# Gated linear attention in one pass: queries and keys scaled by VectorE out of PSUM, and matmuls laid on quadrants of the array

## The chip, the cores and the metric

The kernel runs on one core of one Trainium2 chip. The metric is the device time of one execution in microseconds (us). Engines are named as the profile names them: PE is TensorE, DVE VectorE, ACT ScalarE, POOL GpSimd, SP SyncE. L1649 is line 1649 of the kernel.

## The reference, cut to what matters

The kernel computes a whole decoder of four layers on x of 32 sequences x 128 positions x 128 features, in float32. The change touches one sublayer, the attention of layer 2: a gated linear attention with 16 heads of 64 and chunks of 64 positions, so two chunks a sequence.

```python
def chunk_gla(q, k, v, alpha, C=64):          # q and k were scaled to length one per head
    log_a = jnp.log(jnp.maximum(alpha, 1e-06))
    la_cum = jnp.cumsum(log_a, axis=3)
    la_mean = la_cum.mean(-1)
    decay = jnp.exp(la_mean[..., :, None] - la_mean[..., None, :]) * tril
    attn_intra = jnp.einsum('bhncd,bhnmd->bhncm', q, k) * decay
    o_intra = jnp.einsum('bhncm,bhnmd->bhncd', attn_intra, v)
    decay_to_end = jnp.exp(la_cum[:, :, :, -1:, :] - la_cum)
    kv_chunk = jnp.einsum('bhncf,bhnce->bhnfe', k * decay_to_end, v)
    q_dec = q * jnp.exp(la_cum)
    ...                                        # state S, from zero: o = q_dec @ S, then S * chunk_decay + kv_chunk
    return (o_intra + o_inter).reshape(B, Hh, N, D)
```

The state starts at zero and there are two chunks, so chunk 0 needs o_intra alone, and chunk 1 adds its decayed queries times kv_chunk of chunk 0. q, k, v and the gate are projections of the layer-normalised x to 1024 columns. alpha is a sigmoid, and its logarithm is made as -ln(1 + exp(-g)). The result is projected back to 128 features, and x is added.

## The kernel before, in words

All layers run one after the other; each ends with a barrier over all engines. The attention of layer 2 is the function gla. The function decoder calls it through chunks("c", ...), once for each of PASSES = 4 groups of NB = 8 sequences ("batches"); between the calls lies the barrier.

A call first normalises its eight batches: DVE computes statistics and applies them with scale and shift (lines 68 to 91), ACT takes the root (L107), PE transposes (L59), ACT copies the result into xt_c (L1705). Only then does the loop start.

The loop is software-pipelined by a list written out by hand. ORDER (in the head of gla) goes over c and names for each c the steps of three batches: the front part of batch c + 2, the middle of c + 1, the back of c. Names in capitals are units: PE writes a unit's result into a pair of PSUM banks, of which there are four in a ring, so unit k waits until the pair of unit k - 4 was freed. Every engine walks the same list in order and does its own part of each name; each serves its queue strictly in that order. The units of a period are G, QD, Q, QT, S1, K, KT, ES, O, DF, V, OT, SC, OUT:

- G, Q, K, V (L1649): projections of one batch, two matmuls of 512 columns each. The profile shows two records for each float matmul that is not a transposition.
- For Q and K, ACT squares out of PSUM (SQ, L1716); DVE copies the raw values out (QN, KN, L1819), which frees the pair, and sums the squares per head (L1820) and clips (L1823). After both, ACT takes Ln (L1724) and Exp (L1729), which gives RN, one over the length; POOL multiplies QN and KN by it (L1794).
- For G, DVE adds the bias and clips (L1809, L1811), ACT takes Exp and Ln (L1719, L1722), DVE negates and clips (L1826) and sums per head (L1831, into LM).
- QT, KT (L1655): eight transposes each of the scaled queries and keys; ACT and DVE copy them out (L1741, L1836).
- ES (L1659): cumulated log gates by a matmul with a constant; ACT's Exp makes EX; POOL multiplies queries and keys with it into KQ (L1783, L1785).
- DF (L1664): differences of the means; ACT's Exp and POOL's triangle (L1788) make DEC.
- SC (L1670): scores; DVE multiplies by DEC (L1844, L1845). QD (L1675) transposes the decayed queries of chunk 1; S1 (L1679) makes the state of chunk 0.
- O (L1687, L1688): the output of both chunks; ACT copies it (L1762), OT (L1692) transposes it, DVE copies (L1855), OUT (L1696) projects, DVE adds x (L1858).

## Time and profile before

| | us |
|---|---|
| median of 3 runs | 4913.18 (4910.89 to 4914.86) |
| the profiled execution | 4913.76 |
| its span | 4912.0 |
| the layer, from its first to its last instruction | 847.2 |

The span is the time from the first to the last instruction. The layer lies from 2169.8 to 3017 us in it. In timelines a row is a run of equal instructions (x is their count), merged; the number behind the start is the time from the first one's start to the last one's end, so with PE, whose matmuls overlap, the distance between starts of neighbouring rows tells what a unit costs. A bracket at the end gives the idle time before a row and what ended it.

### The profile page before, as it was taken

To read this page: it belongs to the slowest core of one execution; us is meant where nothing else is said; L and a number is where in the kernel's file an instruction comes from. 1 tells how busy PE (TensorE), PEld (TensorE's weight loads), DVE (VectorE), ACT (ScalarE), POOL (GpSimd) and SP (SyncE) were. 2 spreads that over 40 slices of the span, in tenths; PEclk is the share of its full clock that TensorE was granted. 3 is DMA by queue.
4 is the path that set the end of the run, shared out by engine and by line. 5 is a ranking of instruction groups with operands and counts; after the bars stand their busy time and mean duration, and the time that the engine had idled before them with its cause. 6 is when DMAs were issued, how large, how long until landed. Compare 5 with 4: busy or idle time off the path is not lost. (4 is left out here: it accounts for less than half of the span.)

```text
span 4912.0 us, 79412 instructions
## 1 busy us (share of the span) xinstructions
PE 3958.9 (81%) x30626; PEld 2747.9 (56%) x30626; DVE 3057.8 (62%) x7919; ACT 2146.5 (44%) x3375; POOL 1238.5 (25%) x803
## 2 busy tenths in 40 slices
PE   0788888787998789879898897654549999598998
PEld 0466666565565566646565655443436777365665
DVE  9577777566899567577666674985352112466545
ACT  4466666443222245436565465541123344354222
POOL 2444444222343211015454453321000000010000
PEclk9999999997999679889999998776579999799999
DMA  2222222000000010000000000003300000000000
GB/s 87 49 48 48 49 47 42 4 1 1 1 1 1 1 50 2 1 1 1 1 1 1 1 1 1 14 20 109 99 13 1 1 1 1 27 2 2 1 1 18
DMA packets 58267, 91.98 MB, mean 19 GB/s; under 512 B 15410, under 2 KB 42500, under 8 KB 56132
## 3 DMA queue, kind: packets, MB, share of 16 engines
q1 hardware_dynamic: 53620, 80.09, 7.0%
q10 hardware_dynamic: 4272, 6.81, 0.4%
q8 instruction: 245, 4.01, 0.3%
q14 instruction: 130, 1.06, 0.1%
HBM read 42.69 MB, written 10.62 MB: 11 GB/s over the span
## 5 line engine op out<-in xcount | busy, mean ns | idle before, releaser
L844 PE MATMUL banks<-XT,weight_region 128*128 128x512 f32 x1696 | 798.0, 610 | 0.0
L866 PEld LDWEIGHTS banks<-weight_region,HT 128*128 128x128 f32 x4672 | 576.8, 196 | 136.9 <-issue 111.1
L1123 DVE SCALAR_TENSOR_TENSOR x_res<-banks,WT,x_res 128x128 f32<-128x128 f32 x1056 | 297.4, 344 | 519.8 <-PE banks L866 466.6
L866 PE MATMUL banks<-weight_region,HT 128*128 128x128 f32 x4672 | 581.7, 280 | 14.2 <-DVE HT L1111 8.7
L844 PEld LDWEIGHTS banks<-XT,weight_region 128*128 128x128 f32 x1696 | 312.0, 197 | 295.3 <-issue 290.6
L945 ACT ACTIVATE HT<-banks,weight_region 128x512 f32<-128x512 f32 x256 | 174.3, 687 | 269.3 <-PE banks L844 263.0
L1649 PE MATMUL banks<-weight_region,xt_c 128*128 128x512 f32 x512 | 256.1, 631 | 5.9 <-DVE KNT L1836 3.2
L458 DVE TENSOR_REDUCE MX<-banks 128x8 f32<-128x1152 f32 x128 | 173.2, 1353 | 115.6 <-PE banks L275 113.7
L384 ACT COPY PT<-banks 128x384 f32<-128x384 f32 x384 | 171.5, 481 | 132.0 <-PE banks L285 130.3
L1502 ACT COPY PT<-banks 77x512 f32<-77x512 f32 x256 | 143.1, 582 | 189.4 <-PE banks L1424 189.4
L999 POOL TENSOR_TENSOR T<-T,T 128x512 f32<-128x512 f32 x128 | 162.9, 1274 | 216.5 <-ACT T L968 214.2
L968 ACT ACTIVATE T<-T 128x512 f32<-128x512 f32 x128 | 80.4, 630 | 275.9 <-DVE T L1100 275.8
L59 PE MATMUL banks<-sb_c_ident,XN 128*128 128x128 f32 x96 | 26.5, 432 | 200.8 <-DVE XN L91 163.9
L961 ACT ACTIVATE T<-banks 128x512 f32<-128x512 f32 x128 | 76.1, 597 | 244.1 <-PE banks L844 244.0
L285 PE MATMUL banks<-sb_c_ident,SM 128*128 128x128 f32 x1152 | 178.4, 282 | 4.6 <-ACT PT L384 2.7
L427 POOL TENSOR_TENSOR KT<-KT,FL 128x512 f32<-128x512 f32 x64 | 81.3, 1271 | 373.4 <-DVE FL L447 373.4
L1513 POOL MEMSET VZ<- 77x4160 f32 x2 | 7.1, 3562 | 663.7 <-POOLq L48 663.7
L258 PE MATMUL banks<-XT,weight_region 128*128 128x256 f32 x512 | 144.0, 411 | 29.0 <-ACT PT L384 24.8
L399 ACT ACTIVATE SM<-SM 128x1152 f32<-128x1152 f32 x128 | 150.3, 1174 | 29.2 <-DVE SM L466 29.2
L1424 PE MATMUL banks<-sb_c_ident,SM 128*77 128x128 f32 x1024 | 162.3, 293 | 0.0
L1086 DVE TENSOR_TENSOR HT<-banks,T 128x512 f32<-128x512 f32 x128 | 87.9, 690 | 111.9 <-PE banks L844 98.2
L466 DVE TENSOR_TENSOR SM<-banks,MX 128x1024 f32<-128x1024 f32 x128 | 155.4, 1214 | 0.0
(452 smaller groups left out, 9137.8 us busy)
## 6 DMA issues: line engine op xcount, KB each, us to landing
FL<-RAW SPq DMA_DIRECT2D x512, 64.0 KB, 2.3
T<-s4d_k_dram SPq DMA_DIRECT2D x8, 1024.0 KB, 6.0
weight_region<-in_l_ffn__w_dram SPq DMA_DIRECT2D x2, 2048.0 KB, 7.7
film_dram<-F SPq DMA_DIRECT2D x8, 512.0 KB, 2.9
weight_region<-in_l_ffn__w_dram ACTq DMA_DIRECT2D x2, 2048.0 KB
film_out<-film_dram SPq DMA_DIRECT2D x3, 1024.0 KB, 6.5
x_res<-in_x_dram SPq DMA_DIRECT2D x1, 2048.0 KB
weight_region<-in_l_ffn__w_dram SPq DMA_DIRECT2D x2, 1024.0 KB, 9.7
```

The costliest lines, as they stand in the source:

```text
L285: ins = nc.tensor.transpose(ring(item, n)[:, q * P:(q + 1) * P], SM[:, n % 3, 3 * c + q, :], E.ident)
L384: nc.scalar.copy(PT[:, n % 2, 3 * c:3 * c + 3, :].rearrange("p h q -> p (h q)"), ring(f"T{c}", n)[:, 0:3 * P]).then_inc(s.pt, 1)
L399: nc.scalar.activation(SM[:, n % 3], SM[:, n % 3], ACT.Exp, scale=SCALE).then_inc(s.ex, 1)
L458: nc.vector.tensor_reduce(MX[:, n % 2], sc, AXX, ALU.max).then_inc(s.mx, 1)
L466: nc.vector.tensor_tensor(SM[:, n % 3, 1:9, :].rearrange("p (a i) k -> p i a k", a=2), sc[:, :, :, 0:P], bc(MX[:, n % 2].unsqueeze(3), [P, ...
L844: nc.tensor.matmul(PS[:, q % 4, :], w, xt, start=True, stop=True).then_inc(s.h_ps, 1)
L866: ins = nc.tensor.matmul(PS[:, 4 + u % 2, b * P:(b + 1) * P], HT[:, u % 2, j, b * P:(b + 1) * P], w2[j], start=j == 0, stop=j == len(w2) - 1)
L945: ins = nc.scalar.activation(HT[:, u % 2, j, :], PS[:, (first[u] + j) % 4, :], ACT.Gelu, bias=W.b1[:, e, j:j + 1]).then_inc(s.act_done, 1)
L999: nc.gpsimd.tensor_tensor(T1[:, k % 2, :], T1[:, k % 2, :], T2[:, k % 2, :], ALU.mult).then_inc(s.gs, 1)
L1123: ins = nc.vector.scalar_tensor_tensor(R[:, t, :], PS[:, 4 + u % 2, b * P:(b + 1) * P], WT[:, t, e:e + 1], R[:, t, :], ALU.mult, ALU.add)
L1424: ins = nc.tensor.transpose(bank_of("T", k)[0:L, c * P:(c + 1) * P], SM[:, t % 3, 4 * c + a, :], E.ident)
L1649: ins = nc.tensor.matmul(pr[:, a * 512:(a + 1) * 512], E.xt[:, t * P:(t + 1) * P], w[:, a * 512:(a + 1) * 512], start=True, stop=True)
```

## The change

gla is called once and goes over all 32 batches; layer norm becomes three more names in ORDER, once for four batches: st (DVE statistics), ap (ACT: Ln and Exp for the root, POOL a small product, ACT four scalings) and X (PE transposes, ACT applies scale and shift per partition, since features are partitions then). E.r is no longer a chunk of r_all.

The weights of the four projections are reordered on the host so that the even heads fill columns 0 to 511 and the odd ones 512 to 1023 ("halves" o = 0, 1). The units Q and K become K1 and K2, each with four matmuls whose stationary operand is one chunk of 64 positions: K1 holds the keys of chunk 0 and the queries of chunk 1, on swapped partition halves for odd heads, and K2 the rest. ACT squares them, DVE sums and clips, ACT takes Ln and Exp for each alone (r1, r2), and DVE multiplies out of PSUM into T1 and T2 (r1, r2), which is what frees the pair of banks. T1 and T2 are transposed (units of the same names), and ACT copies both out. KQ is one product of T1 and EX on POOL. V, ES and DF write their second half in two column halves of the array, so that odd heads lie on swapped partitions. SC, QS (in place of QD and S1) and O consist of matmuls of 64 x 64 with 64 columns, spread over the four quadrants of the array; O is computed transposed, its second part behind a wait of PE for its own semaphore o1, and OT is DVE's copy of it. There are 12 units a period and not 14, and one X in four periods. ACT preloads one table set for Exp and Ln. The log gates keep their positive sign, the constants carry the minus; the clip of the gate changes its bound so that the later clip is not needed. The memsets go, since no operand is padded with zeros any more.

```diff
@@ -1584,112 +1584,160 @@
...
-    ORDER = []
-    for c in range(-2, NB):
-        for n, t in (("G", c + 2), ("QD", c), ("Q", c + 2), ("QT", c + 1), ("S1", c), ("K", c + 2), ("e", c + 2), ("KT", c + 1),
-                     ("ES", c + 1), ("O", c), ("l", c + 2), ("DF", c + 1), ("r", c + 2), ("V", c + 2), ("OT", c), ("SC", c + 1), ("OUT", c)):
-            if 0 <= t < NB:
...
+    ORDER = [("st", 0), ("ap", 0), ("X", 0)]
+    for c in range(-2, B_ALL):
+        for n, t in (("G", c + 2), ("QS", c), ("K1", c + 2), ("T1", c + 1), ("r1", c + 2), ("e", c + 2), ("K2", c + 2), ("T2", c + 1), ("r2", c + 2), ("l", c + 2),
+                     ("ES", c + 1), ("O", c), ("s", c + 2), ("DF", c + 1), ("V", c + 2), ("SC", c + 1), ("OUT", c), ("rt", c + 2)):
+            if 0 <= t < B_ALL:
                 ORDER.append((n, t))
...
+        for n, lead in (("st", 3), ("ap", 2), ("X", 1)):
+            if (c + 2 + lead) % GB == 0 and 0 < (c + 2 + lead) // GB < NG:
+                ORDER.append((n, (c + 2 + lead) // GB))
...
+                    elif n in ("K1", "K2"):
+                        kc = 0 if n == "K1" else 1
+                        for o in range(2):
+                            for w, k_ in ((W.wk, kc), (W.wq, 1 - kc)):
+                                ins = nc.tensor.matmul(pr[rows(k_ ^ o), cols(o)], chunk[k_], w[:, cols(o)], start=True, stop=True)
+                    elif n == "V":
+                        nc.tensor.matmul(pr[:, cols(0)], x, W.wv[:, cols(0)], start=True, stop=True)
+                        for k_ in range(2):
+                            ins = nc.tensor.matmul(pr[rows(1 - k_), cols(1)], chunk[k_], W.wv[:, cols(1)], start=True, stop=True)
+                    elif n in ("T1", "T2"):
+                        pe.wait_ge(s.n1 if n == "T1" else s.n2, t + 1)
+                        src = (T1 if n == "T1" else T2)[:, t % 2]
                         for j in range(NJ):
                             ins = nc.tensor.transpose(pr[:, j * P:(j + 1) * P], src[:, j * P:(j + 1) * P], E.ident)
-                    elif n == "ES":
...
+                    elif n in ("ES", "DF"):
+                        if n == "ES":
+                            pe.wait_ge(s.lg, t + 1)
+                            m, v = E.gla_sum, LA[:, t % 2]
+                        else:
+                            pe.wait_ge(s.rt, t + 1)
+                            m, v = E.gla_after, RT[:].rearrange("p h c -> p (h c)")
+                        nc.tensor.matmul(pr[:, cols(0)], m, v[:, cols(0)], start=True, stop=True)
+                        for k_ in range(2):
+                            ins = nc.tensor.matmul(pr[rows(1 - k_), cols(1)], m[:, rows(k_)], v[:, cols(1)], start=True, stop=True)
...
+                            for o in range(2):
+                                for key, query, b in ((T1T, T2T, o), (T2T, T1T, 1 - o)):
+                                    ins = nc.tensor.matmul(pr[rows(b), HALF * o + C * j:HALF * o + C * (j + 1)],
+                                                           key[rows(o), j, rows(b)], query[rows(o), j, rows(b)], start=True, stop=True)
...
+                    elif n == "QS":
+                        pe.wait_ge(s.kqd, t + 1)
+                        pe.wait_ge(s.va, t + 1)
+                        for j in range(NJ):
+                            for o in range(2):
+                                at = HALF * o + D * j
+                                nc.tensor.matmul(pr[rows(o), C * j:C * (j + 1)], KQ[rows(1 - o), at:at + D], E.ident[rows(1 - o), rows(1 - o)], start=True, stop=True)
+                                ins = nc.tensor.matmul(pr[rows(o), HALF + D * j:HALF + D * (j + 1)], KQ[rows(o), at:at + D], VA[rows(o), t % 2, at:at + D],
+                                                       start=True, stop=True)
                     elif n == "O":
...
+                            for k_ in (1, 0):
+                                for o in range(2):
+                                    at = HALF * o + D * j
+                                    ins = nc.tensor.matmul(pr[rows(o), HALF * k_ + C * j:HALF * k_ + C * (j + 1)], VA[rows(k_ ^ o), t % 2, at:at + D],
+                                                           AT[rows(k_ ^ o), o, j, :], start=k_ == 0 or j == 0, stop=k_ == 0)
+                        ins.then_inc(s.o1, 1)
+                        pe.wait_ge(s.o1, t + 1)
+                        for j in range(NJ):
+                            for o in range(2):
+                                ins = nc.tensor.matmul(pr[rows(o), HALF + C * j:HALF + C * (j + 1)], S1[rows(o), j, :], QDT[rows(o), j, :],
+                                                       start=False, stop=j == NJ - 1)
...
+                nc.scalar.preload_act_table_set(EXP_LN)
...
+                        nc.scalar.activation(SQ[:, 0], pr, ACT.Square).then_inc(s.sq1, 1)
...
+                    elif n == "r1":
+                        act.wait_ge(s.mx1, t + 1)
+                        nc.scalar.activation(SS[:, p, 0], SS[:, p, 0], ACT.Ln, scale=2.0 ** 40).then_inc(s.ls1, 1)
+                        act.wait_ge(s.ls1, t + 1)
                         if t >= 2:
-                            act.wait_ge(s.kn, t - 1)
...
-                        nc.scalar.activation(RN[:, p], SS[:, p], ACT.Exp, scale=-0.5, bias=E.ln2_20[:]).then_inc(s.rn, 1)
...
+                        nc.scalar.copy(VA[:, p], pr).then_inc(s.va, 1)
...
+                        nc.gpsimd.tensor_tensor(KQ[:].rearrange("p (o j d) -> p o j d", o=2, d=D), by_half(T1[:, p]),
+                                                EX[:].rearrange("p (o j d) -> p o j d", o=2, d=D), ALU.mult).then_inc(s.kqd, 1)
...
-                            nc.gpsimd.tensor_tensor(x, x, bc(RN[:, p, i, :].unsqueeze(2), [P, H, D]), ALU.mult).then_inc(done, 1)
...
-                        nc.vector.tensor_copy((QN if n == "Q" else KN)[:, p], pr).then_inc(s.qc if n == "Q" else s.kc, 1)
...
+                    elif n == "r1":
+                        dve.wait_ge(s.rn1, t + 1)
+                        if t >= 2:
+                            ready(dve, ("T1", t - 2))
+                            dve.wait_ge(s.kqd, t - 1)
+                        nc.vector.tensor_tensor(by_half(T1[:, p]), pair(("K1", t)).rearrange("p (o j d) -> p o j d", o=2, d=D),
+                                                bc(RN[:, p, 0, :].rearrange("p (o j) -> p o j", o=2).unsqueeze(3), [P, 2, NJ, D]), ALU.mult).then_inc(s.n1, 1)
...
+                        nc.vector.tensor_copy(OT[:].rearrange("p j (k c) -> p k j c", k=2), pr.rearrange("p (k j c) -> p k j c", k=2, c=C)).then_inc(s.ot, 1)
...
-                        nc.vector.tensor_tensor(AT0[0:C], prh[0:C], DEC[0:C], ALU.mult)
-                        nc.vector.tensor_tensor(LH[C:P], prh[C:P], DEC[C:P], ALU.mult).then_inc(s.at, 1)
...
+                        nc.vector.tensor_tensor(AT[:].rearrange("p o j c -> p (o j c)"), pr, DEC[:].rearrange("p h c -> p (h c)"), ALU.mult).then_inc(s.at, 1)
...
-        chunks("c", ("l2_attn", gla, nothing))
+        run("l2_attn", gla)
...
-    c["a_gla_sum"] = (same & np.where(q < 64, p > q, p <= q)).astype(f)
+    c["a_gla_sum"] = -(same & np.where(q < 64, p > q, p <= q)).astype(f)
```

## Rows read from the trace of the kernel before

**Rows 1.** Page, part 1: busy time (share of the span) and instructions of each engine.
```profile
PE 3958.9 (81%) x30626; PEld 2747.9 (56%) x30626; DVE 3057.8 (62%) x7919; ACT 2146.5 (44%) x3375; POOL 1238.5 (25%) x803
```
**Rows 2.** Windows of the layer: stretch, us, busy per engine, granted clock, DMA share, GB/s.
```profile
2169.80:2391.00 221.20, 187.80 (x1676) 125.80 (x1676) 148.09 (x177) 125.10 (x137) 111.18 (x54) 0.94 0.00 1
...
sum 847.20, PE 745.30 PEld 501.02 DVE 560.55 ACT 494.93 POOL 426.93; mean PE 186.32 PEld 125.26 DVE 140.14 ACT 123.73 POOL 106.73
```
**Rows 3.** Timeline of PE, one steady period: start us, us, engine, line, operation.
```profile
2308.51 1.08 PE L1675 MATMUL banks<-sb_c_ident,KQ 64*64 64x64 f32 x16
...
2311.34 1.04 PE L1655 MATMUL banks<-sb_c_ident,QN 128*128 128x128 f32 x8
2312.31 2.08 PE L1679 MATMUL banks<-V,KQ 128*64 128x64 f32 x32
2314.31 1.98 PE L1649 MATMUL banks<-weight_region,xt_c 128*128 128x512 f32 x4
2316.14 1.04 PE L1655 MATMUL banks<-sb_c_ident,KN 128*128 128x128 f32 x8
2317.01 1.88 PE L1659 MATMUL banks<-LA,sb_a_gla_sum 128*128 128x512 f32 x4
2318.82 0.27 PE L1687 MATMUL banks<-V,AT 128*64 128x64 f32 x1
...
2320.84 1.98 PE L1664 MATMUL banks<-RT,sb_a_gla_after 128*128 128x512 f32 x4
...
2325.34 1.97 PE L1670 MATMUL banks<-QB,KNT 128*64 128x128 f32 x32
2327.91 2.02 PE L1696 MATMUL banks<-weight_region,OT 128*128 128x128 f32 x16 [0.60 <-DVE OT L1855]
2329.76 1.88 PE L1649 MATMUL banks<-weight_region,xt_c 128*128 128x512 f32 x4
2331.58 1.08 PE L1675 MATMUL banks<-sb_c_ident,KQ 64*64 64x64 f32 x16
```
**Rows 4.** Timelines of ACT and DVE in that period: the norm of the queries.
```profile
2311.54 1.03 ACT L1716 ACTIVATE SQ<-banks 128x1024 f32<-128x1024 f32 x1 [0.91 <-PE banks L1649]
...
2312.60 1.23 DVE L1819 COPY QN<-banks 128x1024 f32<-128x1024 f32 x1 [0.21 <-ACT SQ L1716]
2313.74 1.21 DVE L1820 TENSOR_REDUCE SS<-SQ 128x16 f32<-128x1024 f32 x1
...
2319.78 0.18 DVE L1823 TENSOR_SCALAR SS<-SS 128x32 f32<-128x32 f32 x1
...
2324.34 0.22 ACT L1724 ACTIVATE SS<-SS 128x32 f32<-128x32 f32 x1
...
2326.79 0.31 ACT L1729 ACTIVATE RN<-SS,sb_c_ln 128x32 f32<-128x32 f32 x1
```
**Rows 5.** Groups of instructions by line: busy us, mean ns | idle before, releaser.
```profile
L1722 ACT ACT_TABLE_LOAD x32 | 41.1, 1283 | 0.6
...
L1472 ACT ACT_TABLE_LOAD x2 | 2.6, 1283 | 4.5 <-PEq L48 4.5
...
L1785 POOL TENSOR_TENSOR KQ<-KN,EX 64x1024 f32<-64x1024 f32 x32 | 77.6, 2424 | 2.5
```
**Rows 6.** Timeline of DVE: first G, last result of pass 1, first G after.
```profile
2186.30 1.23 DVE L1809 TENSOR_TENSOR LA<-banks,weight_region 128x1024 f32<-128x1024 f32 x1 [5.66 <-PE banks L1649]
...
2381.24 0.29 DVE L1858 TENSOR_TENSOR weight_region<-banks,x_res 128x128 f32<-128x128 f32 x1 [2.21 <-PE banks L1696]
...
2398.52 1.22 DVE L1809 TENSOR_TENSOR LA<-banks,weight_region 128x1024 f32<-128x1024 f32 x1 [5.66 <-PE banks L1649]
```
**Rows 7.** Timeline of PE in other layers: four row groups, four column groups.
```profile
514.51 0.77 PE L275 MATMUL banks<-KT,QT 32*128 32x144 f32 x16
...
1904.16 0.40 PE L1439 MATMUL banks<-PT,OZ 77*32 77x128 f32 x8
1904.38 0.40 PE L1437 MATMUL banks<-PT,VZ 77*32 77x128 f32 x8
```

## What the change should do to the time, predicted before it was run

> **What bounds the kernel now.** I read the page's busy shares first [rows 1]: PE is busy for 81% of the span, but that is a mean over a dozen layers, and the change touches one. The windows over that layer come next. It takes 847.2 us in four passes of eight batches, and PE is busy for 745.3 us of it, DVE for 560.6, ACT for 494.9, POOL for 426.9 [rows 2]; per batch that is 23.3, 17.5, 15.5 and 13.3 us. In the first pass the granted clock is 0.94, so most of it runs at 2.4 GHz.
>
> A busy PE can still wait, so I laid out one steady period from the timeline of PE, start of unit to start of unit [rows 3]. The unit QD starts at 2308.51 and again at 2331.58: a batch costs 23.07 us. Inside it the units stand shoulder to shoulder: a projection (four records of 512 columns) takes 1.82 us (G, 2329.76 to 2331.58), eight transposes 0.97 (2311.34 to 2312.31), S1 2.00 (2312.31 to 2314.31), ES 1.81 (2317.01 to 2318.82), O 2.02 (2318.82 to 2320.84), OUT 1.85 (2327.91 to 2329.76). The only gap is the 0.60 us before OUT. So in the steady state PE's own work is the bound; what DVE, ACT and POOL do matters only where it comes too late for PE.
>
> The second cost is the ramp. The first evacuations of G in two successive passes lie at 2186.30 and 2398.52 [rows 6]: 212.22 us, against 8 x 23.07 = 184.56. Each pass thus pays 27.66 us for its layer norm in front, for filling and for draining: the last result of the first pass is written at 2381.24, and 17.3 us pass before the next evacuation of G. Four ramps are 110.6 us. Check: 32 x 23.07 + 110.6 = 848.8, against 847.2 measured.
>
> **The change, part by part.**
>
> *One pass in place of four.* Layer norm goes into the loop (units st, ap, X, once in four batches), and three of the four ramps go: 3 x 27.66 = 83.0 us. Of the one that stays, the front gets shorter, because one group of four batches has to be normalised ahead of the first projection and not two. I take 21 us for the ramp; its ends are 28 (as now) and 16. What X costs PE in return is four transposes a group, 1.08 us, so 0.27 us per batch. ACT and DVE do the rest of the norm after their last unit of an iteration and ahead of the next G, with several us to spare.
>
> *PE's list.* The units OT, Q, K, QT, KT become K1, K2, T1, T2; OT goes, because O is now computed already transposed; QD and S1 become one unit QS. By the rows of before [rows 3]: G, K1, K2 at 1.82 are 5.46. V, ES and DF keep their columns, but their second half is issued as two column halves, which changes the tiling of the array once more inside the unit. Where a full unit is followed by a tiled one now, eight transposes take 0.97 us, against 0.87 before a full unit (2316.14 to 2317.01), so I add 0.1 to each: 3 x 1.92 = 5.76. T1 and T2 are 2 x 0.97 = 1.94, OUT 1.85, X 0.27. Sum: 15.28.
>
> *The quadrant units QS, SC and O.* Their matmuls are 64 x 64 with 64 columns, laid out over all four quadrants of the array. There are 32, 32 and 48 of them, and a float matmul leaves two records: 64, 64 and 96. No row of before shows four 64 x 64 tiles at once. The rows nearest to it are of three kinds. One tile at a time: S1, 32 records in 2.00 us, 62.5 ns each. Two column halves at once: O, 64 records in 2.02 us, 31.6 ns each [rows 3]. Four at once: 16 records of 144 columns in four row groups, in 0.77 us of which the last 0.28 is one record's own duration, 31 ns a record, and eight records on four column groups every 0.22 us, 27.5 ns a record of 128 columns [rows 7]. Both of the last are what the columns alone cost when four run together (128 columns on four tiles), so four tiles do run together, by rows as by columns, and the ends of my price are 14 ns (64 columns at that rate) and 62.5 ns. I take 17 ns, one slot of about 66 ns for four, near the 60 ns that a slot of two takes in O. QS and SC are then 64 x 17 = 1.09, with the switch 1.15 each. O has 64 records at 17 (1.09), a wait of PE for its own semaphore (a drain, about 0.3, the duration of one record), then 32 records on two quadrants only, 32 x 30 = 0.96: 2.3 with rounding down. Together 4.6.
>
> *The wait that is new.* Today the PSUM pair of Q or K is freed by a DVE copy that runs right behind SQ [rows 4]. In the change it is freed by the product r1 (or r2), behind a chain over two engines. The ring has four pairs, so the pair of K1 is wanted by ES, and that of K2 by DF. Count from the end of K1: ACT starts SQ 0.20 later (2311.34 to 2311.54) and needs 1.03; DVE reduces, 1.21, and clips, 0.18; ACT's Ln 0.22 waits at most for T1's copy, which ends at 2.25 while the clip ends at 2.65; Exp 0.31; then r1 on DVE, for which the copy out of PSUM of the same size stands, 1.23 [rows 4]. With 0.04 for each handing over that is 4.5, and 0.15 more until PE starts: 4.65. PE meanwhile has T1, K2, T2: 3.76. So PE stands for 0.9 us ahead of ES, in every period. Queued behind r1 on DVE is K2's reduction, and ACT runs e between; K2's chain ends about 8.5 us after K1, and DF is due at about 10.7, so that one costs nothing. The bounds of this stall are 0 and about 2.9 (below).
>
> *What else moves.* ACT loses the table loads, 1.28 us each, 32 of them on L1722 alone [rows 5]; a preloaded table set covers Ln and Exp in another layer, that of L1472, with 2 loads in all [rows 5]. It also loses the copy of O and a half of V's. DVE loses a copy, the negation of LA and half of S1. POOL loses the two normalising products, and its two products into KQ, 2.4 us each [rows 5], become one. I make that about 14, 11 and 7 us per batch for DVE, ACT and POOL, so none of them becomes the bound. I cost these savings at nothing, because PE covers them today and still does. The latest of their results is AT, which needs POOL's DEC: ACT has its part at about 12.0 us after K1's end, and one product of POOL's takes 2.4, so DEC is there at 14.4 and AT at 15.7; PE wants it freed for the next K1 at about 19.
>
> *Sum.* 15.28 + 4.6 + 0.9 = 20.8 us a batch, 2.3 less than now. Over 32 batches 666, with the ramp 687, against 847.2: 160 us less. The profiled execution took 4913.76 us, 0.6 above the median of the three runs and 1.8 above its own span; 4913.76 - 160.6 = 4753.
>
> **The rivals.**
>
> *A: the chain ahead of ES is longer.* It passes ACT, DVE, ACT, DVE, and both serve their queues strictly in order: if S1's copy or the clip of G is late, K1's reduction is late, and e or T1's copy can slip in ahead of Ln. One such slip is a unit of about 1 us on each engine, 2 us together: a stall of 2.9, a period of 22.8, 32 x 22.8 + 21 = 751, time 4817. For it: two slips would be enough. Against it: each engine is idle for a third of the period. Chance 0.17.
>
> *B: the quadrants run in pairs and not in fours.* In QS and O the two row halves of the array write the same PSUM bank, on different partitions; in the four-row-group rows each group has a bank of its own [rows 7], so nothing in the trace shows this sharing. If it keeps them apart, the rate is that of two tiles, 31.6 ns. QS and SC are 2.02 each, O 3.03 + 0.3: 7.4 in place of 4.6, a period of 23.6, 776 in all, time 4842. Chance 0.20. The Trainium skill speaks for it: its page TensorEngine Tiling (Array Packing), Restrictions and Gotchas, says that different row tiles cannot access the same PSUM bank at the same time; by that rule a kernel with this layout would lose the concurrency in QS and O. No row here bears on it either way.
>
> *C: slower than before.* The quadrant records run one after another at the 62.5 ns of S1. 224 records are then 14.0 us and not 4.3, the period 30.5, the layer 997, the time 5064. It decides against the change from a period of 25.8 on, where 32 periods and the ramp are 847: that is 5.0 us over 224 records, about 42 ns for each on average. For it: no row has four quadrants. Against it: rows and columns overlap separately in the trace, so both mechanisms would have to fail. Chance 0.05.
>
> **How the numbers follow.** Forecast 0.55: 4753, its own range 4710 (no stall, quadrants at 14 ns, a ramp of 16) to 4790 (a stall of 1.7, a ramp of 28). A 0.17, B 0.20, C 0.05; 0.03 for the rest, split between much better and no change. To leave out no more than 2 in 10 the range must take in B: 4710 to 4850. Faster by over 0.2% (about what a measurement of this kernel can tell from no change) 0.93, within it 0.02, slower 0.05.
>
> **What would show it.** In the profile after: no second layer norm front inside the layer; in the timeline of PE, QS and SC of 1.1 to 1.2 us each (2.0 would be B, 4.0 C) and O of 2.3; an idle time of about 0.9 us on PE ahead of ES, ended by DVE's r1 (2.9 would be A) and none ahead of DF; ES, V and DF no longer than 1.92; one table load for the layer; POOL near 7 us a batch. What would make the prediction wrong at its root is a period set by something other than PE, or a full-array unit that gets longer because its halves are tiled.

## The result, and the profile after

The changed kernel takes 4756.65 us (median of 4 runs, 4754.77 to 4757.61) against 4914.02 before: a ratio of 0.9677, 95% interval 0.966 to 0.9693, 157.4 us less. The prediction said 4753. Its profiled execution took 4756.02 us with a span of 4754.2.

The layer now runs from 2166.8 us to 2858.7 us: 691.9 us, against 847.2 [rows 2]. That is 155.3 of the 157.4 us. First the window over it (columns as in [rows 2]), which answers to the four passes of before:

```profile
2166.80:2860.00 693.20, 654.56 (x9440) 348.01 (x9440) 383.48 (x490) 356.92 (x506) 212.23 (x106) 0.99 0.01 2
```

PE is busy for 94% of it, and the granted clock is 0.99, so nearly all of it runs at 2.4 GHz. Per batch DVE, ACT and POOL are busy for 12.0, 11.2 and 6.6 us; the prediction had 14, 11 and 7. Next the timeline of PE, one period from the end of K1 to the end of the next K1, with the unit X in it. It answers to [rows 3]:

```profile
2397.52 1.09 PE L1697 MATMUL banks<-sb_c_ident,T 128*128 128x128 f32 x8
2398.55 1.94 PE L1688 MATMUL banks<-weight_region,XT 128*64 128x512 f32 x8
2400.41 1.09 PE L1697 MATMUL banks<-sb_c_ident,T 128*128 128x128 f32 x8
2402.03 1.12 PE L1705 MATMUL banks<-LA,sb_a_gla_sum 128*128 128x512 f32 x2 [0.52 <-DVE T L1905]
...
2404.10 1.16 PE L1733 MATMUL banks<-AT,VA 64*64 64x64 f32 x64
2405.35 1.15 PE L1739 MATMUL banks<-QDT,S 64*64 64x64 f32 x32
2406.43 1.12 PE L1705 MATMUL banks<-RT,sb_a_gla_after 128*128 128x512 f32 x2
...
2408.49 1.12 PE L1690 MATMUL banks<-weight_region,XT 128*128 128x512 f32 x2
...
2410.55 0.27 PE L1714 MATMUL banks<-T2T,T1T 64*64 64x64 f32 x1
...
2411.65 2.05 PE L1744 MATMUL banks<-weight_region,OT 128*128 128x128 f32 x16
2413.53 0.60 PE L59 MATMUL banks<-sb_c_ident,XN 128*128 128x128 f32 x4
2415.10 1.95 PE L1683 MATMUL banks<-weight_region,XT 128*128 128x512 f32 x4 [0.96 <-ACT XT L1769]
2416.98 0.27 PE L1722 MATMUL banks<-sb_c_ident,KQ 64*64 64x64 f32 x1
...
2418.07 1.94 PE L1688 MATMUL banks<-weight_region,XT 128*64 128x512 f32 x8
2419.94 1.09 PE L1697 MATMUL banks<-sb_c_ident,T 128*128 128x128 f32 x8
```

From 2397.52 to 2419.94 are 22.42 us. The loop has seven such periods with an X in it (the first of the eight X stands ahead of the loop); the others take 20.79. There are two waits. One of 0.52 us stands ahead of ES and is ended by DVE's product r1, the other of 0.96 us ahead of G and is ended by ACT's XT, once a group. The list of PE's waits between 2200 and 2800 us has no third one (columns: us in total, times, longest us):

```profile
PE banks L1705 <- DVE T L1905: 14.8, 28, 0.6
PE banks L1683 <- ACT XT L1769: 6.7, 7, 1.0
```

The quadrant units: SC from 2410.55 to 2411.65 is 1.10 us for 64 records, 17.2 ns each; QS from 2416.98 to 2418.07 is 1.09.

Against a period of before (23.07 us) one without X is 2.28 us shorter. By the starts of the units, QS takes 1.9 us less than QD and S1 did, SC 0.9 less, and OT's 0.97 is gone; O takes 0.3 more, V, ES and DF together 0.85 more, and the projections and transposes of queries and keys 0.3. A wait of 0.5 to 0.6 us a period is in both timelines, in different places.

### The profile page after: what moved, and what is told of

Read it like the earlier page. It is cut to its first block and busy times, and to the rows that moved or that the text cites. A ratio compares the mean times of both kernels' runs of the same rounds, so it can differ in the third digit from the quotient of the medians.

```text
span 4754.2 us, 84550 instructions
## 1 busy us (share of the span) xinstructions
PE 3864.8 (81%) x33378; PEld 2592.2 (55%) x33378; DVE 2881.2 (61%) x7807; ACT 2006.8 (42%) x3345; POOL 1023.8 (22%) x703
## 5 line engine op out<-in xcount | busy, mean ns | idle before, releaser
L1843 POOL TENSOR_TENSOR KQ<-T,EX 128x1024 f32<-128x1024 f32 x32 | 75.5, 2359 | 427.9 <-ACT EX L1824 427.9
L285 PEld LDWEIGHTS banks<-sb_c_ident,SM 128*128 128x128 f32 x1152 | 127.9, 141 | 47.3 <-ACT RAW L369 13.6
```

Of the source, the lines that this page charges most:

```text
L285: ins = nc.tensor.transpose(ring(item, n)[:, q * P:(q + 1) * P], SM[:, n % 3, 3 * c + q, :], E.ident)
```

## The experiments

The layers ahead of this one are the same in all kernels, but in the traces of the experiments this layer starts anywhere from 2165.4 (reorder) to 2176.1 us (before_noneg). Differences of a few us between medians therefore say little; I read small effects off the period, the distance between two results that DVE writes, which repeats within 0.02 us in most kernels.

**four_passes.** gla is called for groups of 8 batches again; its list ends with the eighth (not shown).

```diff
-        run("l2_attn", gla)
+        chunks("c", ("l2_attn", gla, nothing))
```

> The changed kernel with its one pass over 32 batches cut into four passes of 8, as before; all else as changed. The prediction gave 27.66 us to each ramp that goes, and 7 us to a shorter front. The trace of the changed kernel shows less: the layer takes 692.8 us, of which 32 periods of 21.2 us (three of 20.79 to one of 22.42) are 678, so one ramp costs about 15 us. Theory 1 (a ramp of the new loop costs what the trace leaves for it, 15 us, plus a barrier and a front, some 5 us): 3 x 20 = 60 us more than the changed kernel, 4817. Theory 2 (a ramp costs what it cost before, 27.66 us): 83 us more, 4840. If it costs under 20 us, the single pass was no part of the gain.

Measured: 4807.46 us, ratio 0.9789 (0.9772 to 0.9805), 50.8 us above the changed kernel. These are the first results of the first two passes, on DVE:

```profile
2225.04 0.29 DVE L1931 TENSOR_TENSOR weight_region<-banks,x_res 128x128 f32<-128x128 f32 x1 [0.35 <-PE banks L1744]
...
2409.53 0.29 DVE L1931 TENSOR_TENSOR weight_region<-banks,x_res 128x128 f32<-128x128 f32 x1 [0.35 <-PE banks L1744]
```

From the first result of a pass to that of the next are 184.49 us, of which eight periods are 167.95 (seven of 20.79, one of 22.42): a ramp is 16.5 us. Before it was 27.4 by the same count, 211.94 less 184.56. In the new loop three ramps are thus 50 us. The layer itself, 737.1 us, is 45 us longer than with one pass and not 50, since four passes have only four periods with X and not seven. Theory 1 is near: it asked for 60, theory 2 for 83. The new loop's ramp is shorter than the old one's even in four passes, by 11 us. Most of that is its front: from the layer's first instruction to the first evacuation of G are 9.6 us in the changed kernel (2166.82 to 2176.46), and 16.5 before (2169.79 to 2186.30).

**pool_norm.** DVE copies the raw values out of PSUM ahead of the sum, POOL multiplies.

```diff
+                        nc.vector.tensor_copy(by_half(T1[:, p]), pr.rearrange("p (o j d) -> p o j d", o=2, d=D)).then_inc(s.c1, 1)
...
+                        nc.gpsimd.tensor_tensor(by_half(T1[:, p]), by_half(T1[:, p]),
+                                                bc(RN[:, p, 0, :].rearrange("p (o j) -> p o j", o=2).unsqueeze(3), [P, 2, NJ, D]), ALU.mult).then_inc(s.n1, 1)
...
-                        nc.vector.tensor_tensor(by_half(T1[:, p]), pair(("K1", t)).rearrange("p (o j d) -> p o j d", o=2, d=D),
-                                                bc(RN[:, p, 0, :].rearrange("p (o j) -> p o j", o=2).unsqueeze(3), [P, 2, NJ, D]), ALU.mult).then_inc(s.n1, 1)
```

The same is done for the second tile, T2. The banks are then free after the copies, and PE waits for those where it waited for the products.

> The changed kernel, but with queries and keys scaled as before: DVE copies K1 and K2 out of PSUM right after the squares, which frees the banks, and POOL multiplies T1 and T2 by RN. Theory 1 (PE bounds, and the product out of PSUM is what makes PE wait ahead of ES): the 0.52 us ahead of ES goes in 28 to 32 periods, 15 us less than the changed kernel, 4741, though POOL gets 3.8 us a batch more. Theory 2 (the product on DVE is part of the gain, because POOL is late with KQ or DEC): slower than the changed kernel by 10 us or more, with PE waiting for DEC or KQ.

Measured: 4746.33 us, ratio 0.9661 (0.9647 to 0.9675). The wait ahead of ES is gone, the period without X is 20.0 to 20.2 in place of 20.79, and the layer from its first instruction to its last result is 20 us shorter; the medians show 10 of it, and the layers ahead take part of the rest (this layer starts 2.5 us later here). Theory 1 holds. The step that gives the change its short description, the scaling by DVE out of PSUM, costs some 0.7 us a period in this order of units; what gains is the rest of the change.

**reorder.** Other places for V, T1 and T2, and a third buffer for V (its index and the two waits of ACT that follow from the new order are not shown).

```diff
-        for n, t in (("G", c + 2), ("QS", c), ("K1", c + 2), ("T1", c + 1), ("r1", c + 2), ("e", c + 2), ("K2", c + 2), ("T2", c + 1), ("r2", c + 2), ("l", c + 2),
-                     ("ES", c + 1), ("O", c), ("s", c + 2), ("DF", c + 1), ("V", c + 2), ("SC", c + 1), ("OUT", c), ("rt", c + 2)):
+        for n, t in (("G", c + 2), ("QS", c), ("K1", c + 2), ("r1", c + 2), ("V", c + 2), ("K2", c + 2), ("T1", c + 1), ("r2", c + 2), ("e", c + 2), ("l", c + 2),
+                     ("ES", c + 1), ("O", c), ("s", c + 2), ("T2", c + 1), ("DF", c + 1), ("SC", c + 1), ("OUT", c), ("rt", c + 2)):
...
-        LA = sb("LA", [P, 2, HD]); T1 = sb("T1", [P, 2, HD]); T2 = sb("T2", [P, 2, HD]); VA = sb("VA", [P, 2, HD])
+        LA = sb("LA", [P, 2, HD]); T1 = sb("T1", [P, 2, HD]); T2 = sb("T2", [P, 2, HD]); VA = sb("VA", [P, 3, HD])
```

> The changed kernel with another order of the units, G QS K1 V K2 T1 ES O T2 DF SC OUT, and three buffers for V: three units of 4.9 us and not 3.9 then stand between K1 and the unit that takes over its banks. Theory 1 (the wait ahead of ES is the chain from K1's squares to its product, 4.5 us from K1's end): the wait goes, 0.52 us in each of 30 periods, 16 us less than the changed kernel, 4741, and period without X of 20.3. Theory 2 (any order moves the wait to another unit, for K2's chain is as long): no change or slower, 4757 and above.

Measured: 4725.0 us, ratio 0.9619 (0.9606 to 0.9632), 31.6 us less than the changed kernel: twice what theory 1 said. The period is 19.65. PE's timeline of this kernel shows the rest:

```profile
2411.26 1.08 PE L1692 MATMUL banks<-weight_region,XT 128*64 128x512 f32 x4
2412.18 1.89 PE L1688 MATMUL banks<-weight_region,XT 128*64 128x512 f32 x8
2413.99 1.09 PE L1697 MATMUL banks<-sb_c_ident,T 128*128 128x128 f32 x8
2414.92 1.02 PE L1705 MATMUL banks<-LA,sb_a_gla_sum 128*128 128x512 f32 x2
2415.88 1.08 PE L1707 MATMUL banks<-LA,sb_a_gla_sum 128*64 128x512 f32 x4
```

T1, now ahead of a full-array unit, takes 0.93 us where it took 1.03. The full half of ES takes 0.96 (2414.92 to 2415.88) right behind T1, where it took 1.05 behind the wait; that of DF, now right behind T2, is 0.1 shorter as well. V's column halves take 0.92 ahead of K2, which is tiled the same way, where they took 1.0 ahead of SC, and K2 takes 1.81 and not 1.87. Each change of the tiling between neighbours costs 0.05 to 0.1 us, and the new order has fewer; together these make 0.44. T2 with the wait behind it took 1.62 us and now takes 0.93, which is 0.69 more. The sum is the 1.14, within 0.01.

**early_x.** X is put ahead of OUT, and no longer at the end of the iteration.

```diff
+            if n == "OUT" and (c + 3) % GB == 0 and 0 < (c + 3) // GB < NG:
+                ORDER.append(("X", (c + 3) // GB))
...
-        for n, lead in (("st", 3), ("ap", 2), ("X", 1)):
+        for n, lead in (("st", 3), ("ap", 2)):
```

> The changed kernel with the unit X of the layer norm moved ahead of OUT, so that ACT's evacuation of it runs beside OUT and G need not wait. In the trace the first G of each group waits 0.96 us for it, 7 times. Theory 1: 7 us less than the changed kernel, 4750, and the period with X takes 21.5 in place of 22.42. Theory 2 (the wait turns up elsewhere, as the ring of banks shifts by one): no change, 4757.

Measured: 4748.56 us, ratio 0.9666 (0.9653 to 0.9679), 8 us less; the period with X is 21.17 and not 22.42, the others stay at 20.79. Theory 1 holds.

**reorder_x.** The edits of reorder and early_x together.

> The order of reorder together with X ahead of OUT (early_x). In reorder the only waits of PE left are 7 of 0.96 us for ACT's XT. Theory 1 (PE is the bound and nothing else is near): these go and 0.4 us of the ring's shift comes in, 8 us less than reorder, 4717, with a period of 19.65 without X and about 20.1 with it. Theory 2 (the other engines are now close): no gain on reorder, 4725.

Measured: 4720.63 us, ratio 0.9606 (0.9593 to 0.9619), periods of 19.65 without X and 20.04 with it, as expected. It is the fastest kernel here, 36 us below the changed one; the step from reorder is within the scatter of the medians, but shows in the period.

**reorder_x_pool.** The edits of pool_norm in the order of reorder_x.

> The order of reorder_x, with queries and keys scaled as before (a copy on DVE, a product on POOL). In the order of the change, the scaling on POOL made the period 0.7 us shorter, since it frees K1's banks earlier. In reorder_x PE does not wait for those banks. Theory 1 (the way of scaling matters only through that wait): the same as reorder_x, 4721, the period 19.65. Theory 2 (POOL's products cost by themselves, through DVE's instructions that POOL holds back, or a later DEC): 5 us or more above reorder_x, the period above 19.8.

Measured: 4772.81 us, ratio 0.9713 (0.97 to 0.9727): 52 us above reorder_x. Theory 1 is wrong, and theory 2 gives the right sign for the wrong reason. The timelines of PE, DVE and ACT of this kernel, one period:

```profile
2423.91 0.24 PE L1716 MATMUL banks<-T2T,T1T 64*64 64x64 f32 x1 [1.46 <-ACT T2T L1796]
...
2411.67 1.22 DVE L1905 COPY T<-banks 128x1024 f32<-128x1024 f32 x1 [1.26 <-ACT SQ L1781]
2412.81 1.21 DVE L1906 TENSOR_REDUCE SS<-SQ 128x16 f32<-128x1024 f32 x1
...
2419.27 0.22 ACT L1812 ACTIVATE SS<-SS 128x16 f32<-128x16 f32 x1 [1.73 <-DVE SS L1918]
2422.76 1.00 ACT L1796 COPY T2T<-banks 128x1024 f32<-128x1024 f32 x1
```

The copy on DVE stands ahead of the sum, so the sum and ACT's Ln come 1.2 us later. ACT serves its list in order, and V's copy and K2's squares stand behind that Ln, so K2's Ln is late twice over: at 2419.27, 10.65 us after K1's start on PE (2408.62), where reorder_x has it at 8.39 (2421.94 after 2413.55). T2's copy, four places further down in ACT's list, is then too late for SC, and the period is 21.2. POOL's products and DEC are not what PE waits for. So the way of scaling does matter in the better order, where the change's way is 1.5 us a period faster; in the change's own order it is 0.7 slower.

**pairs.** The loops over j and o are swapped in SC and QS.

```diff
-                        for j in range(NJ):
-                            for o in range(2):
+                        for o in range(2):
+                            for j in range(NJ):
```

> The changed kernel with the two inner loops of SC and QS swapped, so that all matmuls of one head half come first and then all of the other: the same 64 records in each unit, but neighbours in the list now use two quadrants and not four (in SC those of one row group). Theory 1 (four quadrants run together only where neighbours in the list lie on four): SC and QS take 2.0 us each in place of 1.09, 1.8 us a period, 58 us in all, 4815. Theory 2 (PE looks far enough ahead to find work for the idle quadrants, or the issue of records is the limit and not the quadrants): within 5 us of the changed kernel, 4757.

Measured: 4804.04 us, ratio 0.9781 (0.9766 to 0.9795), 47.4 us more; the period is 22.28 and not 20.79. Here are rows of PE around the two units: the first record of each, and the unit that follows it (SC stands between V's column halves and OUT, QS between G and K1):

```profile
2405.10 1.08 PE L1692 MATMUL banks<-weight_region,XT 128*64 128x512 f32 x4
2406.11 0.27 PE L1714 MATMUL banks<-T2T,T1T 64*64 64x64 f32 x1
...
2407.95 2.05 PE L1744 MATMUL banks<-weight_region,OT 128*128 128x128 f32 x16
2409.84 1.88 PE L1683 MATMUL banks<-weight_region,XT 128*128 128x512 f32 x4
2411.65 0.27 PE L1722 MATMUL banks<-sb_c_ident,KQ 64*64 64x64 f32 x1
...
2413.49 1.94 PE L1688 MATMUL banks<-weight_region,XT 128*64 128x512 f32 x8
```

SC and QS take 1.84 us each (2406.11 to 2407.95, 2411.65 to 2413.49) in place of 1.1, 29 ns a record, and this is the whole 1.49 us of the period. It is the rate of two tiles: G's four records of 512 columns take 1.81 us, so 64 columns take 57 ns on one tile, and 28 if two work side by side. The same matmuls in another order thus lose most of what four quadrants give, and PE does not make up for the order of its list. Theory 1 holds, with its price a fifth too high.

**full_width.** V, ES and DF as two full matmuls; the odd heads are then fed with the wrong chunk.

```diff
-                        nc.tensor.matmul(pr[:, cols(0)], m, v[:, cols(0)], start=True, stop=True)
-                        for k_ in range(2):
-                            ins = nc.tensor.matmul(pr[rows(1 - k_), cols(1)], m[:, rows(k_)], v[:, cols(1)], start=True, stop=True)
+                        for o in range(2):
+                            ins = nc.tensor.matmul(pr[:, cols(o)], m, v[:, cols(o)], start=True, stop=True)
```

> The changed kernel with V, ES and DF as two full matmuls of 512 columns each, so without column halves; the odd heads then get values and gates of the wrong chunk, so this computes something else in the odd heads. It measures what the column halves cost PE. The prediction gave them 0.1 us a unit; in the trace the three take 2.07 us each from start to start, against 1.88 for G. Theory 1: 0.2 us a unit, 0.6 a period, 19 us less than the changed kernel, 4738. Theory 2 (0.1 a unit as predicted, the rest is something else): 10 us less, 4747.

Measured: 4738.37 us, ratio 0.9643 (0.9629 to 0.9656), 18.3 us less, a period of 20.14. The column halves cost 0.65 us a period, 0.2 a unit, twice what the prediction gave them.

**no_preload.** One line less.

```diff
-                nc.scalar.preload_act_table_set(EXP_LN)
```

> The changed kernel without the preloaded table set, so that ACT loads tables whenever Ln follows Exp or Exp follows Ln: up to six loads of 1.28 us a batch. The prediction cost the loads at nothing, as PE covers ACT. Theory 1 (that holds no more, since Ln and Exp of r1 now stand in the chain that frees K1's banks): two loads come into that chain, the wait ahead of ES grows from 0.5 to about 3.1 us, 2.6 x 32 = 83 us more, 4840, with a wait ahead of DF possible on top. Theory 2 (covered by PE): 4757, with ACT at 19 us a batch.

Measured: 4884.85 us, ratio 0.9944 (0.9929 to 0.9959), 128 us more; most periods without X take 24.4 to 24.6 us. Most of the change's gain is gone. The window of 2200 to 2800 us, and PE's timeline from ES on:

```profile
2200.00:2800.00 600.00, 522.04 (x6954) 268.52 (x6952) 281.54 (x364) 463.44 (x531) 158.11 (x79) 0.92 0.01 2
```

```profile
2404.76 1.12 PE L1705 MATMUL banks<-LA,sb_a_gla_sum 128*128 128x512 f32 x2 [2.62 <-DVE T L1904]
2405.81 1.82 PE L1707 MATMUL banks<-LA,sb_a_gla_sum 128*64 128x512 f32 x4
2407.56 1.99 PE L1733 MATMUL banks<-AT,VA 64*64 64x64 f32 x64
2409.64 1.15 PE L1739 MATMUL banks<-QDT,S 64*64 64x64 f32 x32
```

The wait ahead of ES is 2.62 us, 2.1 more than in the changed kernel, as two loads in the chain should make it (a part of the first hides behind T1's copy). That explains 2.1 of the 3.7 us a period. The other 1.6 follow behind the wait: the column halves of ES take 1.75 us (2405.81 to 2407.56) where they take 1.01, and O's first part 2.08 where it takes 1.25. The granted clock of the window is 0.92 and not 1.00, and from 2407 to 2411 us it is 0.70: for a stretch behind each long wait PE is at 1.2 GHz. Theory 1 was right in its mechanism and a third short in its size.

**before_preload.** This is the kernel before, with the preload in front of its loop.

```diff
                 act.wait_ge(s.zero, 1)
+                nc.scalar.preload_act_table_set(EXP_LN)
```

> The kernel before with one line more: the table set for both Exp and Ln is preloaded ahead of the loop. The prediction cost the table loads of the kernel before at nothing. Its rows speak against that in one place: the 0.60 us of PE's idle time ahead of OUT ended with DVE's OT, which stands behind the sums of LA in DVE's queue, and these waited for ACT's Ln with a table load in front of it. Theory 1 (the loads cost what that wait shows): 0.6 us in each of about 30 periods, 18 us less than before, 4896. Theory 2 (covered, another wait takes its place): 4914.

Measured: 5105.98 us, ratio 1.0394 (1.0379 to 1.0408): 192 us slower than before, by taking work away. Both theories are wrong. ACT's table loads are gone, and the period is 30.7 in place of 23.07. PE waits 6.65 us ahead of OUT, for DVE, 6.05 more than before; OUT itself then takes 3.48 us (2370.02 to 2373.50) in place of 1.85, at a granted clock of 0.57 from 2370 to 2374 us, and that is the rest of the 7.6. The timelines of DVE, POOL and PE in that place:

```profile
2359.11 8.38 DVE L1827 TENSOR_SCALAR LA<-LA 128x1024 f32<-128x1024 f32 x1 [1.96 <-ACT LA L1723]
2367.52 1.22 DVE L1832 TENSOR_REDUCE LM<-LA 128x16 f32<-128x1024 f32 x1
...
2358.53 2.35 POOL L1786 TENSOR_TENSOR KQ<-KN,EX 64x1024 f32<-64x1024 f32 x1
2360.85 2.37 POOL L1789 TENSOR_TENSOR DEC<-DEC,sb_a_gla_tril 128x1024 f32<-128x1024 f32 x1
2363.17 1.91 POOL L1795 TENSOR_TENSOR QN<-QN,RN 128x1024 f32<-128x1024 f32 x1
2365.03 1.91 POOL L1795 TENSOR_TENSOR KN<-KN,RN 128x1024 f32<-128x1024 f32 x1
...
2370.02 3.65 PE L1696 MATMUL banks<-weight_region,OT 128*128 128x128 f32 x16 [6.65 <-DVE OT L1856]
```

DVE's negation of LA starts 0.6 us after POOL has begun a product, and ends 0.55 us after POOL has done that product and the three that follow without a gap (2365.03 + 1.91 = 2366.94). It takes 8.38 us; undisturbed it takes 0.69, as the first one of each pass does. The same place in the kernel before:

```profile
2324.46 0.91 DVE L1826 TENSOR_SCALAR LA<-LA 128x1024 f32<-128x1024 f32 x1 [3.38 <-ACT LA L1722]
...
2322.47 2.35 POOL L1785 TENSOR_TENSOR KQ<-KN,EX 64x1024 f32<-64x1024 f32 x1
2326.97 2.36 POOL L1788 TENSOR_TENSOR DEC<-DEC,sb_a_gla_tril 128x1024 f32<-128x1024 f32 x1 [2.15 <-ACT DEC L1752]
```

There ACT's table loads make DEC come later, and POOL has a gap of 2.15 us. The negation ends 0.55 us after the product ahead of the gap (2322.47 + 2.35 = 2324.82), so it takes 0.91 us. The Trainium skill, SBUF — State Buffer, section Who interferes with whom, says that a tensor_scalar from SBUF to SBUF can use a port pair shared with GpSimd, that the pair is locked for a whole instruction and that the loser fully blocks; the trace agrees, and it adds that the loser stays blocked through a whole run of POOL's instructions.

**before_noneg** and **before_noneg_preload.** The change's edit that removes this negation is made in the kernel before, alone and with the preload. The clip's new bound, the second constant with its sign turned and the waits that follow are not shown.

```diff
-                        nc.vector.tensor_scalar(LA[:, p], LA[:, p], -1.0, LN_MIN, ALU.mult, ALU.max).then_inc(s.la, 1)
...
-    c["a_gla_sum"] = (same & np.where(q < 64, p > q, p <= q)).astype(f)
+    c["a_gla_sum"] = -(same & np.where(q < 64, p > q, p <= q)).astype(f)
```

> The kernel before with one edit of the change alone: the log gates keep their positive sign, the constants carry the minus, the clip of the gate has its bound from the later clip, and DVE's negation of LA (L1826) goes. No preload. Theory 1 (the 0.60 us of PE's idle time ahead of OUT hangs on ACT's Ln, L1826, the sum LM and OT in DVE's queue): OT comes 0.9 us earlier, the wait goes, 0.6 x 30 = 18 us less than before, 4896. Theory 2 (OT is not what is late): 4914.

> The kernel before with both edits: no negation on DVE, and the preloaded table set. The preload alone made 192 us: the negation (a tensor_scalar, SBUF to SBUF) took 8.38 us and not 0.9, from the time at which it started to 0.6 us after POOL's run of products ended, with POOL's five products without a gap. Theory 1 (it is this form of DVE's instruction that is held back while POOL works, and the preload let POOL run without a gap beside it): without the negation the slow state is gone, the period is about 22.5, 4896. Theory 2 (DVE as a whole is held back by POOL's run, whatever its instruction): the sum LM that follows gets the 8 us, and the time stays near 5100.

Measured: 4906.4 us, ratio 0.9982 (0.9973 to 0.9991), and 4875.88 us, ratio 0.9924 (0.9912 to 0.9936). The steady periods are 22.48 and 22.43, as expected of both: the 0.60 us ahead of OUT hung on the negation. Alone the edit brings less than the expected 18 us, since in each pass only the four distances between results that were 23.07 get shorter (4 x 4 x 0.6 = 10 us), and the ramps do not. With the preload the 8.38 us instruction is gone, and with it the period of 30.7; the sum LM takes 1.22 us as ever, so POOL held back this one instruction and not DVE as a whole. Most of the 37 us of this kernel come from its ramps: from the last result of a pass to the first of the next are 62.5 to 64.0 us, before 69.7 to 69.9, and the first result of the layer comes 7 us earlier, 27 us in all. Why the ramps gain by the preload stays open.

## Why the prediction was right, point by point

*PE is the bound, before and after.* Right. The stages are shoulder to shoulder in both timelines, and every edit that took time out of PE's list or out of a wait of PE's moved the period by that amount or more (full_width, early_x, reorder).

*The quadrants.* Right, and this was the term with the widest bounds, 14 to 62.5 ns a record. Taken were 17, measured are 17.2. Rival B did not come true: in SC each row half of the array writes a bank of its own, in QS both write the same two banks, and the units take 1.10 and 1.09 us. At 57 ns for 64 columns on one tile, 17 ns a record also needs more than two tiles at work at a time. B's price had taken SC along, which by B's own condition would have kept its rate. The Trainium skill's rule in TensorEngine Tiling (Array Packing), Restrictions and Gotchas, that different row tiles cannot access the same PSUM bank at the same time, costs no time here, where the two write different partitions. Rival C failed by the same rows; pairs shows that something like B can be had by the order of the matmuls alone.

*O.* It takes 2.33 us, against 2.3, by two errors that cancel: the first 64 records with the drain take 1.25 us and not 1.39, the 32 records on two quadrants 1.08 and not 0.96.

*The new wait.* Right in place, cause and nearly in size: 0.52 us idle, 0.60 counted from the end of T2, against 0.9. The chain took what the sum said. From the timelines of ACT, DVE and PE behind the K1 that ends at 2419.94:

```profile
2420.06 1.02 ACT L1779 ACTIVATE SQ<-banks 128x1024 f32<-128x1024 f32 x1 [1.27 <-PE banks L1688]
...
2421.12 1.22 DVE L1890 TENSOR_REDUCE SS<-SQ 128x16 f32<-128x1024 f32 x1 [1.48 <-ACT SQ L1779]
2422.37 0.17 DVE L1892 TENSOR_SCALAR SS<-SS 128x16 f32<-128x16 f32 x1
2423.17 1.23 DVE L1905 TENSOR_TENSOR T<-banks,RN 128x1024 f32<-128x1024 f32 x1 [0.62 <-ACT RN L1807]
...
2424.45 1.12 PE L1705 MATMUL banks<-LA,sb_a_gla_sum 128*128 128x512 f32 x2 [0.53 <-DVE T L1905]
```

ES starts 4.51 us after K1's end, predicted 4.65. The rest of the difference is that T1, K2 and T2 take 3.91 us and not 3.76. Rival A, a chain longer by 2 us, did not occur; no_preload shows what it would have cost, 3.7 us a period, since the clock falls too. I had priced A without that.

*No wait ahead of DF.* Right, but by less than I thought. I had DF due at about 10.7 us after K1's end; the terms of my own sum (4.65, ES 1.92, O 2.3) give 8.9, and that is what DF does (2406.43 after 2397.52 is 8.91). The product r2 ends 0.55 us earlier, and not 2.2.

*V, ES, DF.* Too low: 2.06 us each where I took 1.92. I had priced one change of tiling at 0.1 us, and full_width measures 0.2 us a unit. A unit that gets longer because its halves are tiled was one of my two signs of being wrong at the root; it came, but costs only 0.4 us a period over the forecast.

*X.* Here is the one wait that the prediction denied. It called X 1.08 us a group and said ACT did its part with several us to spare. By its own rows four transposes are half of 0.97 us, and X itself takes 0.5 to 0.6; but ORDER has it right ahead of the G that reads its result, and G waits 0.96 us for the evacuation. The period with X is 1.63 us longer, and the price that was too high for X hid more than half of the missing wait. The step that failed is "ahead of the next G": being in time for G's place in the list is not enough when nothing stands between.

*The ramps.* Together nearly right. I gave 83 us to three ramps of 27.66 and 6.7 to the shorter front, 90 together. Measured: the one that stays is 15.2 us (691.9 less 25 x 20.79 and 7 x 22.42), so 95 of 110.6 us went. The term that was mis-sized is this ramp, 21 with 16 as its lower end. The front is shorter by 6.9 us, as I took it; I had left filling and draining as they were, and they are 4 to 5.5 us shorter too. How much of the 95 is the single pass depends on the order of counting: 83 if the old loop is put into one pass first, which no run did, and 50 if the new loop is there first (four_passes), with 44 for its four shorter ramps.

*The sum.* A period was to be 20.8 us and is 21.15 on average; the ramp was to be 21 and is 15.2. The errors are +11 and -6 us over the layer. Inside a period the wait, 0.3 too high, offsets most of the 0.4 that V, ES and DF were too low. So 4753 is closer to 4756.65 than the terms deserve, and that part is luck. The lower end of the forecast's own range is misadded: its terms (periods of 19.2 and a ramp of 16, 631 us in all) give 4698 and not 4710.

*ACT's loads and DVE's negation at nothing.* Wrong as said of the kernel before: to take both away is worth 37 us there, the negation alone 6, and the loads alone minus 192. It did not hurt the forecast, because the period after was summed from its own units and not as a difference. But the sentence that PE covers them both before and after was wrong twice, for in the changed kernel the loads would cost 128 us.

## What to carry to other kernels

Where PE is the bound, price a reordered pipeline by laying out the new list unit by unit from the old rows; then look at each unit for the chain that frees the banks it takes, and at each load for the unit that stands right before its reader. Neighbours in the list decide: four quadrants only run together if the list alternates between them, and a change of tiling costs 0.05 to 0.2 us. And before you call an engine's work covered, ask whether its delay keeps two others apart; taking table loads out of an ACT that PE seemed to cover made a kernel 4% slower.

## What the runs showed of the hardware that was not expected

- DVE's tensor_scalar from SBUF to SBUF can be held back through four products of POOL in a row: 8.38 us for 0.69 us of work (before_preload, 24 of the layer's 32 negations). Reductions and copies out of PSUM beside POOL's products kept their 1.2 us.
- A wait of PE of 2.62 us in each period brought the granted clock of the window from 1.00 to 0.92, and the column halves of ES and the first part of O behind it took 1.6 us longer (no_preload). Waits of 0.5 to 1 us did not: the windows of the changed kernel between 2200 and 2800 us show 1.00.
- Quadrants of both row halves that write one PSUM bank on different partitions keep the rate of quadrants with banks of their own: 1.09 us for QS, 1.10 for SC, 17 ns a record of 64 columns.
- The cost of a tiled matmul depends on its neighbours in the list: 17 ns a record with four quadrants in turn (changed kernel), 29 with two (pairs).
